# The end of attention: turns on VectorE and weighing on GpSimd in place of TensorE transposes, in a four-layer transformer kernel

## The chip, the cores and the metric

The kernel runs on one core of one Trainium2 chip (trn2). The metric is device time in microseconds of one launch. A core has TensorE (PE in the profile; its weight loads are PEld), VectorE (DVE), ScalarE (ACT), GpSimd (POOL) and SyncE (SP, which here only issues DMAs). They run side by side, each works through its own list of instructions in order, and they meet at semaphores.

## The reference, cut to what matters

Sixteen sequences of 256 tokens with 256 features pass four decoder layers; all four also look at a context of 77 rows per sequence. There are seven attentions, numbered 0 to 6 in the kernel: 0, 2 and 4 are self attention (0 and 2 causal, 4 with a mask that is handed in), 1, 3, 5 and 6 look at the context. Each has 16 heads of 16 features:

```python
q = x @ wq + bq;  k = ctx @ wk + bk;  v = ctx @ wv + bv      # ctx = x in self attention
scores = einsum('bhqd,bhkd->bhqk', q, k) / sqrt(16)
a = softmax(scores, axis=-1)
o = einsum('bhqk,bhkd->bqhd', a, v).reshape(B, N, 256)
x = x + o @ wo + bo                                          # with layer norms before or after
```

Since the rows of the softmax sum to one, the bias `bv` comes out as `o + bv`, and `(o + bv) @ wo + bo` is `o @ wo + (bv @ wo + bo)`. The layers also hold a feed-forward of 1024 features (two of them) and, in the second, a mixture of 8 experts of which 2 are chosen for each token. All matrices are float32; the scores are made with bfloat16 pieces (three to a number), so that they are as exact as float32 needs.

## The kernel before, in words

The program has three phases, one after the other, each a block with its own buffers. Phase a runs attentions 0 to 3 and the router for all 16 sequences, phase b the experts (39 groups of 256 rows), phase c attentions 4 to 6 and what follows. Within a and c up to seven sequences are under way at once.

The order on each engine is fixed before the program is built. `Plan.step` lists every step with the engine, a cost in microseconds, what it comes after (`after`), and which buffers it takes and gives back. `Plan.run` then plays them through: of all open steps it takes the one that can start first by its own costs, and of equals the more urgent one. The urgency is the length of the way to the end, a bonus for earlier sequences, and a number by stage from the table `AHEAD`, whose stages are named in `STAGES`. The costs, the takes and the table thus set the order; on the chip, each engine works it off and waits where something is late.

The end of one attention, before, in steps (lines of the kernel before):

- `pv` (L744): TensorE multiplies the exponentials with the values, each head's 16 values and a column of ones, so that the sum of the exponentials comes with it. Two steps for an attention, 8 heads each. Four heads stand side by side in the array (32 columns each); the outcome in PSUM has features on the partitions (32 for a head) and tokens along the free side.
- `raw` (L949): ScalarE copies each of the two banks to SBUF, 128x512.
- `turn_raw` (L754): TensorE transposes them, 4 blocks of 128x128 in each of two steps, so that tokens lie on the partitions.
- `recip`, `weigh` (L1112, L1118): VectorE takes the reciprocal of the sums and multiplies, for each half of the tokens.
- `turn_normed` (L763): TensorE transposes the outcome back, 4 blocks.
- `heads` (L955): ScalarE copies to SBUF and adds the value bias, two instructions.
- `out` (L780): TensorE multiplies with `wo`; `add` (L1124): VectorE adds the residual, to which GpSimd has added `bo` (`bias`, L1300) or which carries it in the shift of its layer norm (`shift`, L1290).

Other steps that the text speaks of: `qm` (L708, masks by L841 and L845) makes the scores for their maxima, `max` (L1087) takes these on VectorE, L1093 to L1106 split them in three bfloat16 pieces, `turn_shift` (L716) turns them, `turned_shift` (L931) copies, `shift_in` (L1352) is a DMA into the stack `qs`, and `km` (L728) makes the scores less the maxima; `exp` (L938) follows on ScalarE. `proj` is L686, `value_proj` L695, the feed-forward L796 and L780, the transposing of tokens L677 with the copy L911, and a norm's last step L1069.

## Time and profile before

| what | us |
|---|---|
| runs of the kernel before | 3228.45, 3234.26, 3242.9 (median 3234.26) |
| span of the profiled execution | 3229.7 |
| TensorE busy | 3020.0 (94%) |
| VectorE busy | 1570.3 (49%) |
| ScalarE busy | 1544.5 (48%) |
| GpSimd busy | 872.7 (27%) |
| mean granted clock of TensorE, share of full speed | 0.964 |

The profiled execution has no time of its own beside its span: 3229.7 us from the first to the last instruction, which is 4.6 us under the median of the runs. Phase a fills the span from 0 to about 1490 us, phase b to about 2070, phase c the rest.

A line of the profile names the line of the kernel, the engine, the operation and the tiles (out<-in). A float32 matmul shows as two instructions, so that four of them are an "x8"; a transpose shows as one. The duration of a matmul holds its way through the array and overlaps with the next; what a group of matmuls costs is told by the distance from its start to the start of the next, which is what the chain of waits gives.

### The profile page before, as it was taken

The page shows a single profiled execution, that of the slowest core. Times are in us where ns is not written, and L with a number is a line of the kernel's source. Part 1 is how long each engine was busy: PE and PEld are TensorE (multiplying, and loading weights), DVE is VectorE, ACT ScalarE, POOL GpSimd, SP SyncE. Part 2 cuts the span into 40 slices and gives each one's busy share as a digit, 9 for nine tenths or more (in the row PEclk, how much of TensorE's full clock was granted, in tenths as well). Part 3 has the DMA queues.
Part 4 walks back from the last instruction along what each step waited for, and adds up shares of the span by engine and source line. Part 5 has one row for each costly group of instructions (what it writes and reads, how often), then busy time and mean ns, then how long its engine had stood idle before and what let it go on. Part 6 is the DMA issues. An engine that isn't in the chain of part 4 may idle for free. (4 is left out here: it accounts for less than half of the span.)

```text
span 3229.7 us, 61791 instructions
## 1 busy us (share of the span) xinstructions
PE 3020.0 (94%) x23913; PEld 2459.4 (76%) x24016; DVE 1570.3 (49%) x4057; ACT 1544.5 (48%) x3403; POOL 872.7 (27%) x991
## 2 busy tenths in 40 slices
PE   7899999999999999876999999889999999999996
PEld 5788877788888777764888888656777777777774
DVE  4644454775556655452101011266566666666542
ACT  4555455565555566342222222145556555655552
POOL 2221213333223324222000000242234434433231
PEclk8999999999999999986999999899999999999997
DMA  9743536555645663724676665474435554656241
GB/s 165 110 64 45 62 50 84 96 79 76 79 63 76 81 84 67 193 44 159 209 230 210 199 205 192 98 111 65 51 60 73 77 77 63 82 75 79 40 56 25
DMA packets 394607, 319.34 MB, mean 99 GB/s; under 512 B 151711, under 2 KB 378271, under 8 KB 394303
## 3 DMA queue, kind: packets, MB, share of 16 engines
q1 hardware_dynamic: 371062, 276.77, 48.0%
q0 software_dynamic: 8272, 23.73, 3.0%
q10 hardware_dynamic: 14981, 14.89, 1.6%
q8 instruction: 190, 3.11, 0.5%
q14 instruction: 102, 0.84, 0.1%
HBM read 134.33 MB, written 37.22 MB: 53 GB/s over the span
## 5 line engine op out<-in xcount | busy, mean ns | idle before, releaser
L938 ACT ACTIVATE a_prob<-a_bank 128x512 f32<-128x512 f32 (+1 forms) x640 | 339.0, 599 | 108.7 <-PE a_bank L728 105.2
L1087 DVE TENSOR_REDUCE a_maxima<-a_bank 128x2 f32<-128x512 f32 (+3 forms) x576 | 338.2, 645 | 102.9 <-PE a_bank L708 102.6
L974 ACT ACTIVATE b_group_hidden<-b_bank,b_b 128x256 f32<-128x256 f32 x312 | 131.0, 471 | 421.6 <-PE b_bank L796 421.6
L938 ACT ACTIVATE c_prob<-c_bank 128x512 f32<-128x512 f32 (+1 forms) x512 | 263.2, 599 | 142.2 <-PE c_bank L728 140.4
L1087 DVE TENSOR_REDUCE c_maxima<-c_bank 128x2 f32<-128x512 f32 (+2 forms) x448 | 266.5, 638 | 95.2 <-PE c_bank L708 93.8
L796 PE MATMUL b_bank<-b_group_xt,b_w 128*128 128x256 f32 x1248 | 284.3, 381 | 0.8 <-DVE b_group_xt L1128 0.8
L780 PE MATMUL b_bank<-b_w,b_group_hidden 128*128 128x256 f32 x1248 | 275.8, 379 | 0.9 <-ACT b_group_hidden L974 0.9
L841 PE MATMUL a_bank<-a_causal_b,keep_identb 128*128 128x256 bf16 (+1 forms) x768 | 244.3, 318 | 34.2 <-DMA a_qs<-a_shift 25.0
L780 PEld LDWEIGHTS b_bank<-b_w,b_group_hidden 128*128 128x128 f32 x1248 | 237.0, 190 | 33.5 <-ACT b_group_hidden L974 1.3
L796 PEld LDWEIGHTS b_bank<-b_group_xt,b_w 128*128 128x128 f32 x1248 | 235.6, 191 | 32.0 <-DVE b_group_xt L1128 1.2
L1133 DVE TENSOR_TENSOR b_group_y<-b_bank,b_b 128x512 f32<-128x512 f32 x39 | 27.0, 692 | 364.8 <-PE b_bank L780 364.8
L728 PE MATMUL a_bank<-a_qs,a_ks 99*128 99x128 bf16 x1536 | 148.2, 225 | 0.0
L728 PEld LDWEIGHTS a_bank<-a_qs,a_ks 99*128 99x128 bf16 x1536 | 124.2, 101 | 23.2 <-issue 1.8
L708 PE MATMUL a_bank<-a_ks,a_qs 96*128 96x128 bf16 x1536 | 140.7, 220 | 0.0
L1124 DVE TENSOR_TENSOR a_tok<-a_bank,a_tok 128x512 f32<-128x512 f32 x80 | 55.1, 689 | 170.0 <-PE a_bank L780 169.8
L708 PEld LDWEIGHTS a_bank<-a_ks,a_qs 96*128 96x128 bf16 x1536 | 120.0, 98 | 22.7 <-issue 1.4
L780 PE MATMUL a_bank<-a_at_o,a_heads 128*128 128x256 f32 x512 | 131.2, 401 | 4.3 <-ACT a_heads L955 4.3
L1294 POOL TENSOR_TENSOR a_parts_q<-a_rest,a_parts_q 128x512 bf16<-128x512 f32 x64 | 74.3, 1161 | 224.8 <-ACT a_parts_q L927 224.7
L1286 POOL TENSOR_TENSOR c_tok<-c_tok,weights_row_L_xattn_ln_g 128x512 f32<-128x512 f32 x64 | 81.5, 1274 | 185.1 <-PE c_bank L677 185.1
L949 ACT ACTIVATE a_raw<-a_bank 128x512 f32<-128x512 f32 x128 | 76.4, 597 | 115.1 <-PE a_bank L744 114.5
L686 PE MATMUL a_bank<-a_xt,a_at_q 128*128 128x256 f32 x512 | 126.7, 391 | 3.2 <-ACT a_xt L911 1.6
L796 PE MATMUL c_bank<-c_xt,c_weights_f 128*128 128x256 f32 x512 | 122.4, 383 | 0.8 <-ACT c_xt L911 0.7
(239 smaller groups left out, 6475.9 us busy)
## 6 DMA issues: line engine op xcount, KB each, us to landing
b_w<-in_L_xattn_e_w SPq DMA_DIRECT2D x78, 1024.0 KB, 7.2
a_qs<-a_parts_q SPq DMA_DIRECT2D x384, 128.0 KB, 4.5
c_qs<-c_parts_q SPq DMA_DIRECT2D x288, 128.0 KB, 4.4
a_ks<-a_parts_k SPq DMA_DIRECT2D x192, 128.0 KB, 5.5
c_ks<-c_parts_k SPq DMA_DIRECT2D x96, 128.0 KB, 6.0
b_group_x<-sorted_in SPq DMA_DIRECT2D x39, 256.0 KB, 6.7
sorted_out<-b_group_y ACTq DMA_DIRECT2D x39, 256.0 KB, 5.1
sorted_in<-a_zeros SPq DMA_DIRECT2D x8, 1024.0 KB, 8.7
```

The source lines that it names most:

```text
L686: ins = pe.matmul(bank[:, 0, m * n:(m + 1) * n], weight[:, kt, m * P:(m + 1) * P], xt[:, kt, 0:n], start=(kt == 0), stop=(kt == KT - 1))
L708: ins = pe.matmul(bank[:, 0, to:to + m], qs[0:STACK, h, q * P:(q + 1) * P], ks[0:STACK, h, kt * P:kt * P + m], start=(at in CROSS), stop=( ...
L728: ins = pe.matmul(bank[0:kn, 0, to:to + m], ks[0:STACK + NPART, h, kt * P:kt * P + kn], qs[0:STACK + NPART, h, q0:q0 + m], start=(at in CR ...
L780: ins = pe.matmul(bank[:, 0, q * D:(q + 1) * D], heads[:, kt, q * P:(q + 1) * P], weight[:, kt, :], start=(kt == 0), stop=(kt == kts - 1))
L796: ins = pe.matmul(bank[:, 0, j * S:(j + 1) * S], weight[:, kt, f * P:(f + 1) * P], xt[:, kt, :], start=(kt == 0), stop=(kt == KT - 1))
L841: pe.matmul(blocks, k.identb, k.causal[:, keys_first, :].unsqueeze(1).broadcast_to([P, 4 // step, P]), start=True, stop=False)
L938: act.activation(prob[0:rows, first:first + cols], bank[0:rows, 0, 0:cols], ACT.Exp, scale=SCALE).then_inc(k.own(s), 1)
L949: act.activation(tile(s, "raw"), tile(s, "bank")[:, 0, :], ACT.Copy).then_inc(k.own(s), 1)
L974: ins = act.activation(hidden[:, f, :], bank[:, 0, j * S:(j + 1) * S], ACT.Gelu, bias=b1[:, f:f + 1])
L1087: v.tensor_reduce(maxima[:, q:q + qn, h:h + n].rearrange("p q h -> p h q"), bank[:, 0, 0:cols].rearrange("p (j q n) -> p j q n", j=n, q=qn ...
L1286: pool.tensor_tensor(x, x, over(k.gains[at][0]), ALU.mult).then_inc(k.own(s), 1)
L1294: pool.tensor_tensor(parts[:, 2, :, 0:n], rest[:, :, 0:n], parts[:, 1, :, 0:n], ALU.subtract).then_inc(k.own(s), 1)
```

## The change

The end of an attention now runs in five steps and without TensorE:

- `flip`: VectorE turns the 32x32 blocks of a `pv` bank (128x512) straight from PSUM into the buffer `flat`. As each head has 32 partitions, tokens then lie on partitions within a block. Two for an attention.
- `recip`: one reciprocal on VectorE for the whole attention.
- `weigh`: one multiplication on GpSimd, 128x512 in SBUF, into `normed`.
- `heads`: VectorE turns 32x32 blocks back, 128x512 from SBUF to SBUF. No bias is added.

Each block keeps its head's 16 features, so the order of features differs from before; the rows of `wo` and the value biases are laid out to fit (`paired`). The value bias is multiplied with `wo` once for each attention (`bias_out`, TensorE, two matmuls with the bias spread over the columns) and added to the row that holds `bo` or the norm's shift (`bias_fold`, VectorE). The buffers `raw` (four of 128x512) go, `flat` comes (two of 128x1024). The costs of `pv` in the plan rise, and all numbers of `AHEAD` are others.

```diff
-            plan.step("tensor", "pv", b, at, i, us=1.13 if at in CAUSAL else 1.35 if at in SELF else 0.5,
+            plan.step("tensor", "pv", b, at, i, us=1.3 if at in CAUSAL else 1.74 if at in SELF else 0.87,
...
-            plan.step("scalar", "raw", b, at, i, us=0.65, after=[("pv", b, at, i)], gives=["bank"], bank=pv, raw=raw)
...
-        plan.step("tensor", "turn_raw", b, at, q, us=0.44, after=[("raw", b, at, 0), ("raw", b, at, 1)]
...
-        plan.step("vector", "recip", b, at, q, us=0.28, after=[("turn_raw", b, at, q)], bank=bank, recip=recip)
-        plan.step("vector", "weigh", b, at, q, us=0.45, after=[("recip", b, at, q)] + ([("weigh", b, at, 0)] if q else []),
...
-    plan.step("tensor", "turn_normed", b, at, us=0.44, after=[("weigh", b, at, 0), ("weigh", b, at, 1)], takes=["bank", "heads"],
...
-    plan.step("scalar", "heads", b, at, us=0.87, after=[("turn_normed", b, at)], gives=["bank"],
...
+            plan.step("vector", "flip", b, at, i, us=0.69, after=[("pv", b, at, i)], gives=["bank"], bank=pv, flat=flat)
+    normed, heads, recip = ("normed", lab), ("heads", lab), ("recip", lab)
+    plan.step("vector", "recip", b, at, us=0.28, after=[("flip", b, at, 0), ("flip", b, at, 1)], takes=["recip"], flat=flat, recip=recip)
+    plan.step("gpsimd", "weigh", b, at, us=1.27, lag=0.1, after=[("recip", b, at)], takes=["normed"], gives=["flat", "recip"],
+              flat=flat, recip=recip, normed=normed)
+    plan.step("vector", "heads", b, at, us=0.69, after=[("weigh", b, at)], takes=["heads"], gives=["normed"],
+              normed=normed, heads=heads)
...
+SHIFT_AFTER = {"l1_1": 3, "l1_3": 4, "l2_1": 5, "l2_3": 6}
...
+def value_bias_steps(plan, at, ready, row_ready):
+    bank = ("bank", ("value_bias", at))
+    plan.step("tensor", "bias_out", -1, "bias", at, us=0.87, after=ready, takes=["bank"], bank=bank)
+    plan.step("vector", "bias_fold", -1, "bias", at, us=0.45, after=[("bias_out", -1, "bias", at)] + row_ready, gives=["bank"], bank=bank)
...
+    for at in (0, 1, 2, 3):
+        value_bias_steps(plan, at, [("load", -1, "a", at), ("load", -1, "a", "first")],
+                         [("fold", -1, "a")] if at == 3 else [bias_in(at)])
...
-AHEAD = {"a": {("shifts", 0): 0.1, ("shifts", 1): 2.4, ("shifts", 2): 0.3, ("shifts", 3): 0.8, ("shifts", "l0_ff"): -1.0,
+AHEAD = {"a": {("ends", 0): 0.6, ("ends", 1): 1.0, ("ends", 2): -0.2, ("ends", 3): -2.8, "ends": 0.4,
...
+        elif s.kind == "bias_out":
+            if phase == "a":
+                until.wait_ge(*done("load", -1, "a", s.part))
+                until.wait_ge(*done("load", -1, "a", "first"))
             until.wait_ge(*freed(s, "bank"))
+            bias, weight = k.biases[s.part][2], k.weights[s.part][3]
+            for kt in range(KT):
+                ins = pe.matmul(bank[:, 0, 0:D], bias[:, kt:kt + 1].broadcast_to([P, P]), weight[:, kt, :],
+                                start=(kt == 0), stop=(kt == KT - 1))
...
+        elif s.kind == "flip":
+            flat = tile(s, "flat")[:, s.part, :, :, :].rearrange("p b g c -> p g b c")
+            v.transpose(flat, tile(s, "bank")[:, 0, :].rearrange("p (g b c) -> p g b c", g=2, c=32)).then_inc(k.own(s), 1)
         elif s.kind == "recip":
+            v.reciprocal(tile(s, "recip"), tile(s, "flat").rearrange("p k b g c -> p (k b g) c")[:, :, HD]).then_inc(k.own(s), 1)
+        elif s.kind == "heads":
+            v.transpose(tile(s, "heads").rearrange("p k t -> p (k t)"),
+                        tile(s, "normed").rearrange("p n c -> p (n c)")).then_inc(k.own(s), 1)
...
+        elif s.kind == "weigh":
+            pool.tensor_tensor(tile(s, "normed"), flat[:, :, 0:HD],
+                               recip.unsqueeze(2).broadcast_to([P, recip.shape[1], HD]), ALU.mult).then_inc(k.own(s), 1)
```

First, TensorE at the very start of the program, before (L677 transposes the first tokens, L686 is their projection):

```order
L677 MATMUL a_bank<-keep_identity,a_tok 128x128 x4
L686 MATMUL a_bank<-a_xt,a_at_q 128x256 x4
L686 MATMUL a_bank<-a_xt,a_at_k 128x256 x4
L695 MATMUL a_bank<-a_at_v,a_xt 128x256 x4
L686 MATMUL a_bank<-a_ctx_t,a_at_k 128x77 x4
```

and after (L768 is `bias_out`, L689, L698 and L707 are the former L677, L686 and L695):

```order
L768 MATMUL a_bank<-a_at_o,keep_columns 128x256 x2
L689 MATMUL a_bank<-keep_identity,a_tok 128x128 x4
L698 MATMUL a_bank<-a_xt,a_at_q 128x256 x4
L698 MATMUL a_bank<-a_xt,a_at_k 128x256 x4
L707 MATMUL a_bank<-a_at_v,a_xt 128x256 x4
```

The folding of attention 0's bias, which needs the weights, stands ahead of the first transposing, which needs only tokens and the identity.

Second, the weights of attentions 2 and 3, which are loaded by ScalarE's DMA queue. TensorE after, where L740 and L756 are the former L728 and L744, L786 the former L780:

```order
L740 MATMUL a_bank<-a_qs,a_ctx_ks 77x256 x16
L698 MATMUL a_bank<-a_xt,a_at_q 128x256 x4
L728 MATMUL a_bank<-keep_identb,a_least_parts 96x128 x2
L786 MATMUL a_bank<-a_at_o,a_heads 128x256 x4
L756 MATMUL a_bank<-a_prob,a_ctx_values 32x256 x8
L768 MATMUL a_bank<-a_at_o,keep_columns 128x256 x2
L707 MATMUL a_bank<-a_at_v,a_xt 128x256 x4
L768 MATMUL a_bank<-a_at_o,keep_columns 128x256 x2
```

and ScalarE after, whose exponentials (L944) belong to the scores in the first row above:

```order
L944 ACTIVATE a_prob<-a_bank 77x512
L907 DMA a_at_q<-in_L_xattn_sa_wq 128x2x256
L907 DMA a_at_k<-in_L_xattn_sa_wk 128x2x256
L907 DMA a_at_v<-in_L_xattn_sa_wv 128x2x256
L907 DMA a_at_o<-in_L_xattn_sa_wo 128x2x256
L944 ACTIVATE a_prob<-a_bank 77x512
L907 DMA a_at_q<-in_L_xattn_ca_wq 128x2x256
L907 DMA a_at_k<-in_L_xattn_ca_wk 128x2x256
L907 DMA a_at_v<-in_L_xattn_ca_wv 128x2x256
L907 DMA a_at_o<-in_L_xattn_ca_wo 128x2x256
```

The loads stand between the same exponentials as before; new are the two L768 that stand few rows behind them on TensorE.

Third, TensorE in the even middle of phase c, from the turning of attention 6's maxima (L716) to its first scores (L728), before:

```order
L716 MATMUL c_bank<-keep_identb,c_least_parts 96x128 x2
L845 MATMUL c_bank<-c_weights_mask_q,keep_identb 128x512
L708 MATMUL c_bank<-c_ks,c_qs 128x256 x2
L796 MATMUL c_bank<-c_xt,c_weights_f 128x256 x4
L754 MATMUL c_bank<-keep_identity,c_raw 128x128 x4
L845 MATMUL c_bank<-c_weights_mask_q,keep_identb 128x512
L708 MATMUL c_bank<-c_ks,c_qs 128x256 x2
L754 MATMUL c_bank<-keep_identity,c_raw 128x128 x4
L780 MATMUL c_bank<-c_weights_f,c_qs 128x256 x16
L728 MATMUL c_bank<-c_qs,c_ctx_ks 77x256 x12
```

and after, with L728 and L740 in their places:

```order
L728 MATMUL c_bank<-keep_identb,c_least_parts 96x128 x2
L689 MATMUL c_bank<-keep_identity,c_tok 128x128 x4
L851 MATMUL c_bank<-c_weights_mask_q,keep_identb 128x512
L720 MATMUL c_bank<-c_ks,c_qs 128x256 x2
L851 MATMUL c_bank<-c_weights_mask_q,keep_identb 128x512
L720 MATMUL c_bank<-c_ks,c_qs 128x256 x2
L851 MATMUL c_bank<-c_weights_mask_q,keep_identb 128x512
L720 MATMUL c_bank<-c_ks,c_qs 128x256 x2
L698 MATMUL c_bank<-c_xt,c_weights_at_q 128x256 x4
L698 MATMUL c_bank<-c_xt,c_weights_at_k 128x256 x4
L740 MATMUL c_bank<-c_qs,c_ctx_ks 77x256 x12
```

The block of 16 feed-forward matmuls has moved out from between them, and the transposes L754 are gone.

## Rows read from the trace of the kernel before

**Rows 1.** The page, busy time of each engine over the span.

```profile
PE 3020.0 (94%) x23913; PEld 2459.4 (76%) x24016; DVE 1570.3 (49%) x4057; ACT 1544.5 (48%) x3403; POOL 872.7 (27%) x991
```

**Rows 2.** Stretches: from:to, length, busy time by engine, clock, DMA share, GB/s.

```profile
300.00:1400.00 1100.00, 1057.56 (x9917) 872.65 (x9916) 626.46 (x1757) 609.70 (x1342) 327.46 (x368) 0.98 0.54 81
2580.20:2646.80 66.60, 65.18 (x525) 51.48 (x532) 43.29 (x103) 38.08 (x84) 26.89 (x31) 1.00 0.55 75
```

**Rows 3.** Waits of TensorE: who, for whom, us in total, times, longest.

```profile
PE a_bank L841 <- DMA a_qs<-a_shift: 25.0, 10, 10.2
PE c_bank L728 <- DMA c_qs<-c_shift: 13.2, 3, 7.2
...
PE a_bank L763 <- DVE a_normed L1118: 4.3, 6, 1.1
```

**Rows 4.** Chain of waits in one period of phase c: start, us, what.

```profile
2589.82 0.22 PE c_bank L708 x2
...
2595.80 0.44 PE c_bank L754 x4
...
2604.95 0.40 PE c_bank L708 x2
...
2607.36 1.22 DVE c_least_parts L1106
```

**Rows 5.** Timeline of the start: start, us, engine, line, operation.

```profile
8.00 1.09 PE L677 MATMUL a_bank<-keep_identity,a_tok 128*128 128x128 f32 x4 [8.00 <-DVE a_tok L1069]
9.12 1.02 ACT L911 ACTIVATE a_xt<-a_bank,keep_columns 128x256 f32<-128x256 f32 x2 [1.33 <-PE a_bank L677]
10.50 3.78 PE L686 MATMUL a_bank<-a_xt,a_at_q 128*128 128x256 f32 x8 [1.41 <-DMA a_at_o<-in_L_xattn_m_proj_w]
```

**Rows 6.** Timeline of ScalarE's queue at the loads of attentions 2 and 3.

```profile
145.68 0.58 ACT L938 ACTIVATE a_prob<-a_bank 77x512 f32<-77x512 f32 x1
...
147.87 0.64 ACTq L901 DMA_DIRECT2D a_at_o<-in_L_xattn_sa_wo  x1
...
150.48 0.38 ACTq L901 DMA_DIRECT2D a_at_o<-in_L_xattn_ca_wo  x1
```

**Rows 7.** DMA issues: count, KB, us from issue to landing.

```profile
a_at_o<-in_L_xattn_sa_wo ACTq DMA_DIRECT2D x1, 256.0 KB, 10.1
...
a_at_o<-in_L_xattn_ca_wo ACTq DMA_DIRECT2D x1, 256.0 KB, 10.4
```

**Rows 8.** Groups of VectorE by shape: count, busy us, mean ns, idle before.

```profile
L1069 DVE TENSOR_SCALAR c_tok<-c_tok,c_moments,c_rstd 128x256 f32<-128x256 f32 x160 | 92.5, 619 | 33.6 <-POOL c_rstd L1279 33.4
...
L1069 DVE TENSOR_SCALAR a_tok<-a_tok,a_moments,a_rstd 128x256 f32<-128x256 f32 x128 | 54.7, 468 | 28.4 <-POOL a_rstd L1279 24.2 <-PE a_bank L677 3.6
...
L1118 DVE TENSOR_TENSOR c_normed<-c_bank,c_recip 128x256 f32<-128x256 f32 x96 | 40.7, 424 | 3.2
...
L1128 DVE COPY b_group_xt<-b_bank 128x512 f32<-128x512 f32 x39 | 27.0, 691 | 140.3 <-PE b_bank L677 140.3
...
L1112 DVE RECIPROCAL c_recip<-c_bank 128x16 f32<-128x16 f32 x96 | 24.1, 251 | 61.6 <-PE c_bank L754 61.1
```

**Rows 9.** Groups of GpSimd by shape, as rows 8.

```profile
L1300 POOL TENSOR_TENSOR a_tok<-a_tok,a_row_L_xattn_sa_bo 128x512 f32<-128x512 f32 x16 | 20.4, 1273 | 117.6 <-PE a_bank L677 117.6
```

**Rows 10.** Timeline of the last attention's end.

```profile
3206.59 1.93 PE L744 MATMUL c_bank<-c_prob,c_ctx_values 77*32 77x256 f32 x16 [0.74 <-ACT c_prob L938]
...
3214.06 3.78 PE L780 MATMUL c_bank<-c_weights_at_o,c_heads 128*128 128x256 f32 x8 [0.93 <-ACT c_heads L955]
```

**Rows 11.** Timeline of phase c: the maxima are turned and go to the stack.

```profile
2623.57 0.31 PE L716 MATMUL c_bank<-keep_identb,c_least_parts 128*96 128x128 bf16 x2
...
2624.59 0.75 SPq L1352 DMA_DIRECT2D c_qs<-c_shift  x1
```

**Rows 12.** Chain of waits, phase c: two such transfers, from issue to landing.

```profile
2326.95 8.01 DMA c_qs<-c_shift
...
3197.57 2.74 DMA c_qs<-c_shift
```

More of the change, by code:

```diff
@@ L263, in bias_step @@
 def bias_step(plan, b, at, x, out, source, after=(), takes=(), gives=()):
-    plan.step("gpsimd", "bias", b, at, us=1.27, lag=0.1, source=source, after=list(after) + [bias_in(at)], takes=takes, gives=gives,
+    plan.step("gpsimd", "bias", b, at, us=1.27, lag=0.1, source=source, after=list(after) + [bias_in(at) if at == "l0_ff" else ("bias_fold", -1, "bias", at)], takes=takes, gives=gives,
               x=x, out=out)
@@ L334, in attend_steps @@
               shift=shift, qs=qs)
+    flat = ("flat", lab)
     for g in range(H // 4):
```

123 lines of the change are left out of this document (55 added, 68 removed).

## The prediction

> **What bounds the kernel now.** I read the engines' busy time first: TensorE works 3020.0 of 3229.7 us, no other engine reaches half [rows 1]. A share over the span can hide stages, so the stretches come next. In the middle of phase a (300 to 1400 us) TensorE is busy 1057.56 of 1100 us. In the middle of phase c the kernel is periodic: 66.6 us for a sequence, of which TensorE works 65.18, VectorE 43.29, ScalarE 38.08 and GpSimd 26.89 [rows 2]. So there a microsecond taken from TensorE is a microsecond of the period, as long as nothing else comes late. The chain of waits says the same, as nearly all its pieces in a period are TensorE's; one is VectorE's, 1.22 us for an instruction on 32 columns [rows 4]. Last the waits: for the transfer that carries the maxima into the stack TensorE waits 25.0 us in phase a and 13.2 in c, one of them 10.2 us long; inside an attention's end the waits are short, the largest group 4.3 us in all [rows 3].
>
> **Part 1, the transposes go.** Four transposes of 128x128 hold the chain for 0.44 us [rows 4]. An attention has twelve, there are 7 x 16 = 112 attentions, so 336 x 0.44 = 147.8 us of TensorE go, 84.5 in phase a and 63.4 in phase c. Nothing lies beside them, so all of it counts: the period of phase c should fall from 66.6 by 3 x 1.32 = 4.0 to 62.6 us. Nothing is added to TensorE at an attention's end, the `pv` matmuls are the same.
>
> **Part 2, what it costs elsewhere.** No row shows the 32x32 turn. The nearest is VectorE's copy of a 128x512 bank, 691 ns [rows 8]; this I take, since the turn also reads and writes each element once. The lower end is the 424 ns of a 128x256 multiplication from PSUM (half the elements) [rows 8]; the upper, worked out from the copy, is four times 691, 2.8 us, if the turn read its blocks at a quarter of that rate. The Trainium skill ("Vector Engine (DVE) Microarchitecture Reference", section 3.8, the reshape front-end) says the 32x32 transpose sustains one element per cycle per lane; no row here shows it, and by it the price would be the copy's.
>
> VectorE loses 2 x (251 + 424) ns = 1.35 us an attention and gains two flips, a reciprocal and the turn back, 3 x 0.69 + 0.27 = 2.34 us [rows 8]. That is +1.0 us, so +3.0 in a period: 46.3 of 62.6 us, hidden behind TensorE. ScalarE loses two copies and two bias instructions. GpSimd gains one 128x512 operation, 1273 ns [rows 9], 142 us in all, and has 30.7 of 62.6 us in a period. All this is covered by TensorE's work while the order leaves it time. The way from the last `pv` to `out` becomes 0.69 + 0.27 + 1.27 + 0.69 = 2.9, with five handovers about 3.4 us. I counted TensorE's work between the two in the new order with the trace's own durations: in phase c the even part leaves 32, 21 and 7 us for attentions 4, 5 and 6; in phase a about 20 of 64 attentions have under 4.5 us, the least 2.3 but for the drain. They wait a few tenths each. TensorE's present waits inside the ends of attention, some 11 us (the largest group is the 4.3 of [rows 3]), go. I set the two against each other, at 0; the bounds are -11 and +20.
>
> **Part 3, the value bias.** Seven steps of two float32 matmuls. Three fall where TensorE is short: 3 x 0.87 = +2.6. The three of phase c stand ahead of everything at its start, where TensorE waits for other things: 0. The first stands ahead of the first transposing and waits for all four weights of attention 0. These landed at 10.50 us; the transposing ran at 8.00 [rows 5]. Now: weights 10.5, two matmuls at the start's slow clock 1.9 (half of the 3.78 of four), transposing 1.1, copy 1.0, so the projection starts at about 14.7 and not 10.5: +4. Waits of the first 75 us could take some of it back: 0 to 4.4.
>
> **Part 4, two loads that TensorE now waits for early.** The folding for attentions 2 and 3 stands on TensorE behind one projection, one `out` and one `pv` step from the scores whose first exponentials release the loads. Before, from the start of such an exponential (145.68) the last weights of attention 2 landed at 147.87 + 10.1 = 158.0, those of attention 3 at 150.48 + 10.4 = 160.9 [rows 6, 7]; that is 12.3 and 15.2 us later. TensorE's own work from there to the first folding is 1.75 + 1.73 + 0.11 + 1.73 + 1.0 = 6.3 us, less 0.5 for the start of the exponentials, so it stands for about 6.5 us; between the two foldings lie 2.7 us of work against 2.9 of landing. In the middle of phase a nothing gives that back: +7, bounds 0 (the loads find an idle queue) and 9.
>
> **Part 5, the order anew.** What can be counted: steps of transposes followed straight by bfloat16 matmuls fall from 210 to 85. After some of them the next pair takes 0.40 us and not 0.22 [rows 4], I take a third of 125 x 0.2 us: -8, bounds 0 and -25. The number of runs of `pv` steps stays (198 to 202). What I weigh against it is the room for the maxima's way, from L716 to the first scores of the same attention. From L716 to the DMA's issue it takes 1.0 us [rows 11], and the landing 2.74 us on an idle queue, up to 8.01 on a loaded one [rows 12], so 3.7 to 9. The order before left, in the even part of phase c, 7.1, 6.7 and 10.4 us for attentions 4, 5 and 6; the new one leaves 6.4, 5.8 and 5.2, since the feed-forward block has moved away. In phase a about 24 attentions have under 6 us, 17 before. There 17 such cases waited 25.0 us, 1.5 each [rows 3]; 7 more make 10, and I add 5 for phase c: +15, bounds -25 (the new order happens to meet no full queue) and +50.
>
> **Part 6, the drains.** Where one attention after the other ends the phase, latency counts. From the last `pv` (3206.59 + 1.93) to `out` (3214.06) it was 5.5 us [rows 10], now 3.4; 1.3 of the 2.1 are in part 1 already, the rest five times: -4.
>
> **The sum** is made in the span: 3229.7 - 147.8 + 2.6 + 4 + 7 - 8 + 15 - 4 = 3098.5. The median of the runs lies 4.6 above the span, so 3103 us, 4.1% less.
>
> **Rivals.**
> - *Waits eat the gain* (3150). The room of 5.2 to 5.8 us in phase c turns out short in each period, 1 us twice: 12 x 2 = 24 us more, and as much in phase a. For it: a wait of 10.2 us with a room once enough [rows 3]. Against it: rooms of 6.7 us met only one wait in the even part.
> - *GpSimd in VectorE's way* (3140). The same norm instruction takes 468 ns in phase a and 619 in c [rows 8], where GpSimd is busy 30% (327.46 of 1100) and 40% [rows 2], and the 1.22 us of L1106 [rows 4] fits an instruction held up. At 15 ns for each point and 9 points more, 160 instructions cost 22 us in c and some 15 in a, if none is hidden; most of VectorE's time is, so I give it little. The Trainium skill ("SBUF — State Buffer", section on who interferes with whom) has the rule: a VectorE instruction in a two-port mode, or one with two SBUF inputs, and a GpSimd instruction that reads SBUF shut each other out for a whole instruction; the two rows agree with it.
> - *The new order is better than its rooms* (3060). The waits for the maxima in phase a go (-25 in place of +15).
> - *The turn is slow, and VectorE becomes the bound* (about 3290). The period's VectorE work is 43.3 - 4.05 + 0.8 + 9X, with X the time of a turn. It passes the old 66.6 us at X = 2.95; at 3.3 us phase c loses 16 x 3 = 48 us against before, and phase a, whose 46 of 81 us a sequence grow by 12X - 4.3, just reaches its old length; with the drains 3290. It is slower from X = 3 on, just above my upper end of 2.8, at which it would come out level. Against it: reading and writing is all a turn does.
> - *Nothing comes of it* (3230): TensorE would have to wait 4 us more in each period, with 16 us of VectorE's time free. Only a chain of late flips that hold PSUM banks could do it.
>
> **Chances.** Forecast, 3070 to 3135: 0.62. Better order, 3030 to 3070: 0.13. Waits or GpSimd, 3135 to 3218: 0.18. Within half a per cent (16 us, about what a measurement tells from no change): 0.03. Slower: 0.04. So faster 0.93. The range of 8 in 10 is 3050 to 3175; it takes in part 5's -25 and +50 with the small terms' bounds, and most of both cases next to the forecast.
>
> **What would show it.** Right: no TensorE transposes but L689; TensorE busy less by some 150 us or more; the period in phase c near 62.6 with VectorE at 46; flips of 0.69 us; a wait of about 6 us before L768 near 150 us, and the first projection at 14 to 15 us. Wrong: flips over 1 us; TensorE waits for `heads` of over 20 us in all; waits for the maxima's transfer of over 80 us, against 38 before; a period of over 64 us.

## The result and the profile after

The changed kernel takes 3088.11 us (median of 4 runs, 3081.85 to 3092.99), the kernel before beside it 3232.86: a ratio of 0.955, 95% interval 0.9526 to 0.9574. The profiled run took 3081.85 us, the fastest of the four; its span is 3080.0. The forecast was 3103 us.

The page of the profile after, its line of busy times; it answers to [rows 1].

```profile
PE 2882.7 (94%) x22700; PEld 2320.2 (75%) x22700; DVE 1704.9 (55%) x4064; ACT 1335.1 (43%) x2955; POOL 985.5 (32%) x1103
```

TensorE has 1316 instructions fewer (by its weight loads, 24016 before) and 137.3 us less of busy time, and is still busy 94% of the span. The trace before lacks 103 matmul records; an estimate, at the mean of 3020.0 / 23913 = 0.13 us each, makes the true difference some 150 us. Then two stretches of the trace after, with the columns of [rows 2]: from:to, length, busy time of TensorE, its weight loads, VectorE, ScalarE, GpSimd, granted clock, DMA share, GB/s.

```profile
300.00:1400.00 1100.00, 1038.38 (x9771) 842.74 (x9768) 729.42 (x1848) 540.75 (x1197) 396.39 (x436) 0.96 0.54 84
...
2362.50:2425.00 62.50, 62.18 (x497) 47.58 (x497) 45.91 (x103) 32.73 (x72) 29.62 (x33) 1.00 0.49 80
```

Phase c repeats every 62.2 us, 66.5 before (from one transfer of maxima to the third after it). In a period TensorE waits 0.3 us. Phase a is less full: in its middle TensorE is idle for 61.6 of 1100 us, and its clock is 0.96, not 0.98. The first transposing of phase b shows how long phase a lasted: 1437.8 us, 1505.2 before. From the last one (1975.2, 2042.6 before) to the end are 1104.8 us, 1187.1 before. So phase a gave 67.4 us and phase c 82.3, and phase b nothing.

The waits of TensorE, the trace after; they answer to [rows 3]: who, for whom, us in total, times, longest.

```profile
PE a_bank L689 <- DVE a_tok L1064: 18.6, 15, 3.2
PE a_bank L728 <- DVE a_least_parts L1101: 14.3, 7, 4.7
PE a_bank L740 <- DMA a_qs<-a_shift: 12.8, 5, 3.7
...
PE c_bank L786 <- DVE c_heads L1116: 10.4, 7, 3.2
PE a_bank L847 <- DMA a_qs<-a_shift: 9.3, 6, 4.4
...
PE a_bank L786 <- DVE a_heads L1116: 6.6, 9, 2.1
```

The waits for the maxima's transfer are 22.8 us with the 0.7 of phase c, against some 40 before; those for the new end (`heads`) are 17.0.

The prices, in groups by shape: count, busy us, mean ns, idle before; they answer to [rows 8] and [rows 9].

```profile
L1108 DVE STREAM_TRANSPOSE a_flat<-a_bank 128x512 f32<-128x512 f32 x128 | 89.8, 706 | 61.1 <-PE a_bank L756 60.4
...
L1064 DVE TENSOR_SCALAR c_tok<-c_tok,c_moments,c_rstd 128x256 f32<-128x256 f32 x160 | 87.8, 590 | 18.0 <-POOL c_rstd L1283 17.9
...
L1305 POOL TENSOR_TENSOR a_normed<-a_flat,a_recip 128x512 f32<-128x512 f32 x64 | 67.9, 1061 | 124.6 <-DVE a_recip L1112 115.6 <-DVE a_heads L1116 9.0
...
L1116 DVE STREAM_TRANSPOSE a_heads<-a_normed 128x512 f32<-128x512 f32 x64 | 44.9, 701 | 31.5 <-POOL a_normed L1305 20.2 <-PE a_bank L786 11.2
...
L1112 DVE RECIPROCAL a_recip<-a_flat 128x32 f32<-128x32 f32 x64 | 22.5, 352 | 1.9
```

The turn takes 706 ns (0.69 us was taken), the weighing 1061 (1273), the reciprocal 352 (270).

### The profile page after: what moved, and what is told of

Read it like the earlier page. It is cut to its first block and busy times, and to the rows that moved or that the text cites. A ratio compares the mean times of both kernels' runs of the same rounds, so it can differ in the third digit from the quotient of the medians.

```text
span 3080.0 us, 58767 instructions
## 1 busy us (share of the span) xinstructions
PE 2882.7 (94%) x22700; PEld 2320.2 (75%) x22700; DVE 1704.9 (55%) x4064; ACT 1335.1 (43%) x2955; POOL 985.5 (32%) x1103
## 3 DMA queue, kind: packets, MB, share of 16 engines
q8 instruction: 180, 2.95, 0.5%
## 5 line engine op out<-in xcount | busy, mean ns | idle before, releaser
L944 ACT ACTIVATE a_prob<-a_bank 128x512 f32<-128x512 f32 (+1 forms) x640 | 332.9, 601 | 138.2 <-PE a_bank L740 133.9
L944 ACT ACTIVATE c_prob<-c_bank 128x512 f32<-128x512 f32 (+1 forms) x512 | 262.9, 600 | 126.6 <-PE c_bank L740 125.9
L1082 DVE TENSOR_REDUCE c_maxima<-c_bank 128x6 f32<-128x462 f32 (+2 forms) x448 | 263.2, 632 | 42.4 <-PE c_bank L720 42.0
L786 PE MATMUL b_bank<-b_w,b_group_hidden 128*128 128x256 f32 x1248 | 275.8, 379 | 0.9 <-ACT b_group_hidden L969 0.9
L786 PEld LDWEIGHTS b_bank<-b_w,b_group_hidden 128*128 128x128 f32 x1248 | 237.0, 190 | 33.5 <-ACT b_group_hidden L969 1.3
L786 PE MATMUL a_bank<-a_at_o,a_heads 128*128 128x256 f32 x512 | 133.8, 408 | 10.2 <-DVE a_heads L1116 6.6
L740 PE MATMUL a_bank<-a_qs,a_ks 99*128 99x128 bf16 x1536 | 142.6, 220 | 0.0
L698 PE MATMUL a_bank<-a_xt,a_at_q 128*128 128x256 f32 x512 | 134.6, 409 | 5.3 <-ACT a_xt L917 4.4
L740 PEld LDWEIGHTS a_bank<-a_qs,a_ks 99*128 99x128 bf16 x1536 | 120.5, 98 | 22.2 <-issue 0.8
L1317 POOL DMA_INDIRECT c_pair_y<-sorted_out,keep_rows x64 | 64.1, 1002 | 224.0 <-issue 208.5
L1290 POOL TENSOR_TENSOR c_tok<-c_tok,weights_row_L_xattn_ln_g 128x512 f32<-128x512 f32 x64 | 80.8, 1270 | 163.7 <-PE c_bank L689 163.6
L1108 DVE STREAM_TRANSPOSE a_flat<-a_bank 128x512 f32<-128x512 f32 x128 | 89.8, 706 | 61.1 <-PE a_bank L756 60.4
```

The source lines that it names most:

```text
L698: ins = pe.matmul(bank[:, 0, m * n:(m + 1) * n], weight[:, kt, m * P:(m + 1) * P], xt[:, kt, 0:n], start=(kt == 0), stop=(kt == KT - 1))
L740: ins = pe.matmul(bank[0:kn, 0, to:to + m], ks[0:STACK + NPART, h, kt * P:kt * P + kn], qs[0:STACK + NPART, h, q0:q0 + m], start=(at in CR ...
L786: ins = pe.matmul(bank[:, 0, q * D:(q + 1) * D], heads[:, kt, q * P:(q + 1) * P], weight[:, kt, :], start=(kt == 0), stop=(kt == kts - 1))
L944: act.activation(prob[0:rows, first:first + cols], bank[0:rows, 0, 0:cols], ACT.Exp, scale=SCALE).then_inc(k.own(s), 1)
L1082: v.tensor_reduce(maxima[:, q:q + qn, h:h + n].rearrange("p q h -> p h q"), bank[:, 0, 0:cols].rearrange("p (j q n) -> p j q n", j=n, q=qn ...
L1108: v.transpose(flat, tile(s, "bank")[:, 0, :].rearrange("p (g b c) -> p g b c", g=2, c=32)).then_inc(k.own(s), 1)
```

## Experiments

Beside each run stands its ratio to the kernel before, taken on the same chip, which is what is compared. The three that stand ahead of the last in the table ran on a chip where the kernel before took 3251 us, against 3232 to 3234 on the others. The last three columns are each from one profiled run and are not scaled by chip.

| kernel | median us | ratio, 95% interval | phase a | phase c | period of c |
|---|---|---|---|---|---|
| before | 3232.86 | 1 | 1505.2 | 1187.1 | 66.5 |
| after | 3088.11 | 0.955, 0.9526 to 0.9574 | 1437.8 | 1104.8 | 62.2 |
| new ends, old numbers | 3288.29 | 1.0176, 1.0161 to 1.0192 | 1507.9 | 1231.8 | 71.8 |
| old ends, new numbers | 3386.34 | 1.0462, 1.0433 to 1.049 | 1565.0 | 1280.8 | none |
| transposes put back | 3193.81 | 0.9876, 0.9859 to 0.9893 | 1496.4 | 1164.2 | 66.1 |
| value bias later | 3083.72 | 0.9537, 0.9521 to 0.9553 | 1438.2 | 1100.8 | |
| old numbers, maxima on ScalarE's queue | 3254.08 | 1.0066, 1.0043 to 1.0089 | 1502.8 | 1211.7 | |
| maxima on ScalarE's queue | 3092.72 | 0.9563, 0.9539 to 0.9588 | 1429.9 | 1124.1 | 63.3 |
| turns twice | 3178.81 | 0.9834, 0.9806 to 0.9863 | 1494.8 | 1142.7 | 64.7 |
| weighing on VectorE, order made anew | 3223.77 | 0.9979, 0.9961 to 0.9996 | 1506.8 | 1169.0 | |
| weighing on VectorE, same order | 3120.13 | 0.9603, 0.9585 to 0.9621 | 1454.9 | 1127.2 | 64.4 |
| weighing twice | 3125.90 | 0.9626, 0.9604 to 0.9648 | 1473.7 | 1112.7 | 62.3 |
| old pv costs in the planner | 3255.85 | 1.0018, 1.0004 to 1.0033 | 1504.2 | 1214.2 | |
| maxima on ScalarE's queue, phase a alone | 3073.97 | 0.9507, 0.949 to 0.9525 | 1430.6 | 1104.4 | 62.2 |

Phase a is the time to the first transposing of phase b, phase c that from the last one to the end, both from the trace. "Numbers" are the table AHEAD and the planned costs of the `pv` steps.

**One half of the change alone: the ends.**

```diff
 # the changed kernel, with these of the kernel before
-us=1.3 if at in CAUSAL else 1.74 if at in SELF else 0.87
+us=1.13 if at in CAUSAL else 1.35 if at in SELF else 0.5
-AHEAD = {"a": {("ends", 0): 0.6, ("ends", 1): 1.0, ...
+AHEAD = {"a": {("shifts", 0): 0.1, ("shifts", 1): 2.4, ...
```

> The changed kernel with the table AHEAD and the planned costs of the pv steps of the kernel before. So the ends of attention and the value bias are as after the change, and only the numbers that set the order are the old ones. Theory (the gain is the transposes that left TensorE, and the new order brings only the shorter waits for the maxima's transfer, 22.8 us after against about 40 before): 3088 + 17 = 3105 us, period of phase c within 0.5 us of 62.2, TensorE's waits for a_shift and c_shift together near 40. Rival A (the new numbers bring a large part): 3140 us or more, period over 63.5. Rival B (they bring nothing): 3085 to 3092.

All three missed: 1.8% slower than before, with 336 groups of transposes fewer. The waits of this kernel:

```profile
PE c_bank L844 <- DMA c_qs<-c_shift: 42.3, 10, 6.2
PE a_bank L840 <- DMA a_qs<-a_shift: 31.0, 7, 18.2
...
PE c_bank L733 <- DMA c_qs<-c_shift: 10.0, 4, 5.5
...
PE a_bank L733 <- DMA a_qs<-a_shift: 6.7, 4, 3.7
```

90 us of waits for the maxima against 22.8. One of them, in the chain of waits of the same kernel (start, us, what):

```profile
2551.22 0.60 SPq L1354
2551.86 0.61 SPq L1354
2552.52 8.83 DMA c_qs<-c_shift
2561.39 0.61 PE c_bank L844
2562.00 0.43 PE c_bank L733 x2
2562.43 0.43 PE c_bank L844
...
2564.89 0.22 PE c_bank L844
```

ScalarE had the turned maxima ready at 2550.48, SyncE issued three copies of parts first, and the transfer then took 8.83 us where [rows 12] had 8.01 and 2.74. Behind the wait each of these entries (one matmul of L844, or two of L733) takes 0.43 us, and 0.22 some 3 us later. The stretches around it, and ahead of them the flight of another transfer of the same period, columns as above:

```profile
2500.10:2506.10 6.00, 6.00 (x67) 3.78 (x66) 5.50 (x13) 1.58 (x3) 3.47 (x4) 1.00 0.06 9
...
2541.84:2552.52 10.68, 10.33 (x106) 7.58 (x105) 10.14 (x22) 6.53 (x15) 7.31 (x6) 1.00 0.97 118
2552.52:2561.35 8.83, 3.10 (x26) 2.31 (x22) 5.94 (x11) 2.62 (x6) 5.10 (x5) 0.80 1.22 111
...
2561.30:2564.60 3.30, 3.21 (x12) 1.68 (x13) 0.00 (x0) 1.62 (x3) 0.00 (x0) 0.50 1.30 107
```

The DMA share, last but one in a row, is 1.22 while the transfer is under way: the DMA engines are full. The granted clock, ahead of it, is 0.50 for 3.3 us after the wait of some 6 us: TensorE runs at the lower of its levels, 1.2 GHz. In the changed kernel the three transfers of a period are issued at the starts of these stretches:

```profile
2512.87:2518.87 6.00, 6.00 (x58) 4.24 (x50) 5.53 (x13) 1.87 (x4) 0.93 (x2) 1.00 0.96 104
2533.59:2539.59 6.00, 6.00 (x61) 4.16 (x59) 4.07 (x8) 3.64 (x9) 2.85 (x3) 1.00 0.35 98
2561.80:2567.80 6.00, 6.00 (x39) 5.07 (x37) 5.66 (x13) 2.98 (x7) 3.39 (x4) 1.00 0.10 28
```

0.96, 0.35 and 0.10 of the DMA engines, and TensorE waits for none. The room (TensorE's work between the turning of the maxima and the first scores that need them), which I had counted in the order, was almost the same: 5.5, 5.4 and 6.9 us in the slow order, 6.4, 5.8 and 5.2 in the good one. Within the slow period, too, the transfer of 2500.10 met a share of 0.06 and was not waited for, and the one of 2552.52, with about the same room, met 1.22 and was waited for 5.8 us. So in these periods the room does not tell the two orders apart, and what is on the DMA engines during the flight does. Part of the 5.8 us is also the issue, 2.0 us behind the turned maxima.

**The other half alone: the order.** The same two edits the other way round, on the kernel before.

> The kernel before with the new table AHEAD and the new planned costs of the pv steps, and nothing else. Counted in the order, phase c does not come to a fixed period under these numbers. Theory (the numbers fit the new ends and bring nothing by themselves): 3233 to 3265 us, TensorE busy within 10 us of 3020, since the 336 transposes per output half are all still there. Rival A (the order is worth some 17 us in any kernel, by shorter waits for the maxima): 3216. Rival B (the order carries a third or more of the gain): 3185 or less.

The theory's sign was right and its size was not: 4.6% slower. The waits for the maxima are 73.6 us (four groups, 23.3, 23.0, 14.3 and 13.0). TensorE's busy time is 3089.4 us, 69 more than before, at a mean clock of 0.947, for the same instructions (103 of them have no record in the trace before, which makes some 13 of the 69, an estimate from 0.13 us each). Rival A, an order that is good by itself, is out: the numbers fit one set of steps and costs.

**The transposes put back, in the changed kernel's own order.**

```diff
+            if s.kind == "out" and at in k.weights:
+                for i in range(12):
+                    pe.transpose(bank[:, 0, (i % 4) * P:(i % 4 + 1) * P], k.identf, k.identf)
             for q in range(QT):
```

> The changed kernel in its own order, with twelve 128x128 float32 transposes of the identity put back on TensorE in every attention's output step, behind its waits and ahead of its matmuls, into the same PSUM bank that the matmuls then overwrite. No wait is added. Theory (TensorE bounds the kernel nearly everywhere, so its time on the transposes counts in full): 1344 transposes at 0.11 us, +147.8: 3236 us, the time of the kernel before; period of phase c 62.2 + 3.96 = 66.2. Rival A (some of it lies beside waits for other engines): +110 to +130, 3198 to 3218. Rival B (the gain came from elsewhere): under +80, below 3170.

Rival A comes nearest. The ratio rises by 0.0326, which is 105 us of 3232.9, and not 148. (The phases below add up to 118 us: the profiled run was the slowest of this kernel's four, and that of the changed kernel the fastest of its four.) In phase c the price is nearly full: the period goes from 62.2 to 66.1, +3.9 where 3.96 was expected. In phase a the profile shows +58.6 where 84.5 was. Its middle stretch says why:

```profile
300.00:1400.00 1100.00, 1064.69 (x10099) 882.68 (x10097) 706.78 (x1771) 525.42 (x1166) 380.36 (x419) 0.98 0.53 82
```

The idle time falls from 61.6 to 35.3 us and the clock rises from 0.96 to 0.98: part of the transposes lay in waits for others, and with fewer waits the rest ran faster. And the kernel with all the transposes is still 1.2% faster than before. Between the two kernels, with nearly the same work on TensorE, lie 40 us. No run divides them: they hold the order, but also the shorter way through an end and the copies that ScalarE no longer makes (1544.5 us of busy time before, 1334.5 here). The period of phase c is only 0.4 us shorter than before, 6 us in 16 sequences, while phase c as a whole is 22.9 us shorter and phase a 8.8, so most of it lies elsewhere.

**The early steps of the value bias moved.**

```diff
+BEHIND = {0: ("proj", 0, 0, "k"), 1: ("value_proj", 0, 1, 0), 2: ("turn", 0, "l0_3", 0), 3: ("turn", 0, "l1_0", 0)}
-              takes=["bank"], bank=bank)
+              takes=["bank"], bank=bank, behind=[BEHIND[at]] if at in BEHIND else [])
```

> The changed kernel, in which the four value-bias steps of phase a stand later in TensorE's order: the first behind the first key projection, the third and fourth behind the first transposings of the feed-forward norm and of the second layer, when their loads have long landed. The rest of the order of phase a keeps 96% of its sequence, phase c all of it. Theory (the early steps made TensorE wait 5.2 us at the start and 3.2 + 0.4 us for the loads, with nothing that gives it back): the first projection at 10.5 us again, no wait of over 1 us before the value-bias matmuls, 3088 - 9 = 3079 us. Rival (the waits were covered and come back one step later, for the maxima or for ScalarE): within 3 us of 3088.

The intervals overlap. The waits in question are gone, but phase a is no shorter (1438.2 against 1437.8). They came back as others, in this kernel's waits (4.6 us and none in the changed kernel):

```profile
PE a_bank L702 <- DMA a_ctx_t<-in_ctx_t: 14.2, 4, 9.9
...
PE a_bank L702 <- DMA a_at_v<-in_L_xattn_cv_w: 13.0, 1, 13.0
```

By these waits the start is bound by its loads, wherever TensorE stands while they come. The 4 us are in phase c, whose order was not touched, and so are no effect that this edit explains.

**The maxima's transfer on ScalarE's queue**, under the old numbers and then in the changed kernel.

```diff
 # scalar_program, behind the copy of the turned maxima; SyncE issues it no more
+            until.wait_ge(*done("turned_shift", b, at))
+            into = k.plan.steps["shift_in", b, at, 0]
+            act.dma_start(tile(into, "qs")[STACK:STACK + NPART, :, :], tile(s, "shift")).then_inc(k.own(into), 16)
```

> The kernel with the new ends under the old numbers (measured 3288 us), in which the transfer of the maxima into the stack is issued by ScalarE, right behind its own copy of the turned maxima, and not by SyncE behind the copies of the parts. The order of every other instruction is the same. Theory (with the old numbers the maxima's transfer stands on SyncE's queue right behind three or four copies of 128 KB; its landings of 6.5 and 8.8 us and the slow matmuls behind such a wait are what the order costs): the landings fall toward 3 us, the waits for c_shift and a_shift from 90 to under 30 us, the granted clock from 0.944 to over 0.955: 3180 to 3210 us. Rival A (the 16 DMA engines are shared, so the bytes ahead delay it on any queue): landings of 5 us or more, 3260 to 3290. Rival B (the waits for the maxima are not what makes this kernel slow, it is the short room at the ends): waits for the maxima gone, and waits for heads up by as much, within 20 us of 3288.

By the ratios 36 us come back, of 202; the time lies above the theory's range and just below rival A's. Here are the four longest of its transfers between 2500 and 2800 us, from the chain of waits:

```profile
2545.72 8.75 DMA c_qs<-c_shift
...
2615.77 8.20 DMA c_qs<-c_shift
...
2683.78 8.62 DMA c_qs<-c_shift
...
2752.67 8.81 DMA c_qs<-c_shift
```

On SyncE's queue, under the same numbers, they took 8.12 to 9.29 us. So rival A holds for the landing, and what was won is the issue, which no longer stands behind the copies. The Trainium skill says that each DMA engine takes turns between the queues that have work, a packet at a time ("DMA: Bandwidth & Descriptors", section "Queues, rings and completion order"); from that I had expected a small transfer to land early from a queue of its own. In this case's trace it did not. The waits for the maxima's transfer fell from 90 to 43 us. But 127 us of idle time and 70 of busy time divide the slow order (on SyncE's queue) from the good one, and of the 127 only 67 are waits for that transfer. Of the other 60, 28 are longer waits for VectorE's taking of the maxima (33.3 us against 5.1), 16 for its norms (42.3 against 26.1) and 7 for `heads` (24.0 against 17.0). No run tests what each of them is worth.

> The same edit in the changed kernel: ScalarE issues the maxima's transfer. Theory (TensorE waits for it only 22 us in all here, since the new order leaves the queue free when it comes): 10 to 20 us less, 3070 to 3078. Rival A (the issue holds ScalarE 0.8 to 1.2 us, 112 times, and the exponentials behind it come later): 3090 to 3110. Rival B (the queue was never its delay): within 3 us of 3088.

Level with the changed kernel, and at 3092.72 us inside rival A's range; but its phases are not level: phase a is 7.9 us shorter, phase c 19.3 longer, where nothing was to be won and the period grew from 62.2 to 63.3 us. TensorE now waits six times in 400 us for ScalarE's copy of a transposed norm, 0.5 us each.

**The turns twice.** Each 32x32 turn is issued twice in a row into the same tile.

```diff
 # flip, and the turn back (heads) likewise; again() waits for the first before the second
-            v.transpose(flat, ...).then_inc(k.own(s), 1)
+            for i in range(2):
+                ins = v.transpose(flat, ...)
+                if i < 1:
+                    again(k, v, ins)
+            ins.then_inc(k.own(s), 1)
```

> The changed kernel in its own order, with each 32x32 turn on VectorE done twice in a row into the same tile: two flips and the turn back, 3 x 0.71 = 2.1 us more in an attention, 6.3 us in a period of phase c (45.8 to 52.2 of 62.2 us). The way from the last pv step to the output matmuls grows from about 3.9 to 6.0 us. Theory (VectorE is hidden in the period, the ends are not everywhere: by TensorE's work between the two in the order, the rooms fall short by 51 us more, 40 in phase a, 11 in c): 3088 + 51 = 3139, range 3115 to 3165, period of phase c still 62.2 to 63. Rival A (all is hidden): under 3100. Rival B (VectorE's lateness passes on to the maxima and to the norms, since one more microsecond of VectorE in ten makes each of its answers late): 3190 or more, period over 65.

+91 us, between theory and rival B. A period of phase c, and TensorE's waits in six of them:

```profile
2500.00:2564.70 64.70, 62.40 (x496) 47.35 (x495) 52.59 (x112) 32.93 (x72) 29.67 (x33) 1.00 0.50 77
```

```profile
PE c_bank L689 <- DVE c_tok L1070: 11.3, 7, 1.6
PE c_bank L728 <- DVE c_least_parts L1107: 4.5, 13, 0.4
```

VectorE has 12 us free in a period, and yet 6.3 us more of it cost 2.5. In this even part the waits are not for the ends but for the norm and for the maxima. Outside these periods TensorE does wait for the ends, over the whole run 52.2 us against 17.0:

```profile
PE a_bank L786 <- DVE a_heads L1127: 29.8, 24, 3.4
PE c_bank L786 <- DVE c_heads L1127: 22.4, 11, 5.4
```

The profiled run is 94 us longer than that of the changed kernel. TensorE's idle time is 71 us of it: 35 for `heads`, 20 for the norms, 7 for a bank that a flip holds, the rest in small pieces; its busy time is the other 23. The chain of waits of the changed kernel shows that the maxima were at their limit already:

```profile
2507.06 1.79 DVE c_maxima L1082 x3
...
2508.87 1.29 DVE c_maxima L1082 x2
...
2510.18 0.33 DVE c_least_parts L1088
...
2510.54 1.10 DVE c_least_rest L1092
```

From 2507.04 to 2512.12 the chain runs over VectorE, five microseconds of the period, though TensorE waits only 0.3.

**The weighing twice on GpSimd**, in the same manner.

```diff
-            pool.tensor_tensor(tile(s, "normed"), flat[:, :, 0:HD], ..., ALU.mult).then_inc(k.own(s), 1)
+            for i in range(2):
+                ins = pool.tensor_tensor(tile(s, "normed"), flat[:, :, 0:HD], ..., ALU.mult)
+                if i < 1:
+                    again(k, pool, ins)
+            ins.then_inc(k.own(s), 1)
```

> The changed kernel in its own order, with the weighing on GpSimd done twice in a row into the same tile: 1.06 us more of GpSimd in an attention, 3.2 us in a period of phase c (29.6 to 32.8), and as much more on the way through the end. Theory (only the longer way costs, where TensorE's work in the order does not cover it: 18 us more of shortfall in phase a, 4 in c): 3110, range 3098 to 3120. Rival A (a busier GpSimd also holds VectorE up): 3125 or more, VectorE's operations on 32 columns and its norm instruction longer by 10% or more. Rival B (all hidden): under 3095.

The ratio is 0.0076 over that of the changed kernel: +25 us, 3112 us on the chip of the changed kernel, as the theory had it. The profiled phases are 35.9 us longer in a and 7.9 in c; both hold what the slower chip adds (18 us for the kernel before), so phase a had most of the cost, but how much is not shown. The period is 62.3:

```profile
2500.00:2562.30 62.30, 61.25 (x488) 47.15 (x492) 46.44 (x102) 32.22 (x72) 32.86 (x36) 1.00 0.51 80
```

3.2 us more of GpSimd made VectorE's time 0.9 us longer (45.57 in a period of the changed kernel). The four instructions on 32 columns take 1.41 us in the mean of phase c, where they took 1.25 (13% more, part of rival A's sign); the norm's there stayed at 0.59 us. VectorE is held up, but in phase c that stays hidden. The Trainium skill ("SBUF — State Buffer", section on who interferes with whom) says that a VectorE instruction with two SBUF inputs and a GpSimd instruction that reads SBUF shut each other out for a whole instruction. The rows agree with it, and as a price it is small here.

**The weighing on VectorE**, first with the order made anew by the same numbers, then in the very order of the changed kernel.

```diff
 # first: the planner sees one step on VectorE (heads, 1.3 us), which weighs and turns back
-    plan.step("gpsimd", "weigh", b, at, us=1.27, ...
-    plan.step("vector", "heads", b, at, us=0.69, ...
+    plan.step("vector", "heads", b, at, us=1.3, after=[("recip", b, at)], ...
 # then: the planner sees the steps of the changed kernel, and only the emitted order differs
-            order[s.engine].append(s)
+            order[s.engine if s.kind != "weigh" else "vector"].append(s)
```

> The changed kernel with the weighing done by VectorE ahead of the turn back, and not by GpSimd; the order is made anew by the same numbers and keeps 65 to 74% of its sequence. An estimate of the weighing on VectorE is 0.69 us, by its other instructions on 128x512 elements, so VectorE has 47.9 of 62.2 us in a period and GpSimd 26.4 instead of 29.6. Theory (both engines are hidden, and only the order decides): 3080 to 3130, whichever way the order falls; period near 62.2. Rival A (GpSimd's instructions hold up VectorE's, so taking 112 of them away brings time): 3070 or less, L1092's successor near 200 ns instead of 469 in phase c. Rival B (any order that is not searched for loses as the old numbers did): 3150 or more.

> The changed kernel with the weighing on VectorE, as in the run before, but in the very order of the changed kernel: TensorE, ScalarE and SyncE issue what they did, and the weighing stands in VectorE's order where it stood in the common order of all engines. Theory (what made the run before 136 us slower is the new order that the planner laid, not the engine of the weighing): 3070 to 3105, with 3085 taken: the way through the end of attention is shorter by some 0.4 us (-8), VectorE has 77 us more work (+13, at the 0.17 us per us that doubling the turns leaves beside the ways), GpSimd's 119 us no longer hold VectorE up (-8). Rival A (the weighing belongs on GpSimd, since VectorE's time is short): 3120 or more. Rival B (GpSimd's hold of VectorE is a large cost): below 3065.

Ratios 0.9979 and 0.9603: the first meets rival B, the second is 3104.5 us on the chip of the changed kernel and inside the theory's range. The engine costs 0.0053, 17 us; the order that the planner made of it costs 0.0376, 122 us. In the same order L1092 takes 421 ns in the mean of phase c, 469 in the changed kernel, so GpSimd's hold on it eased little. The period is 64.4 us, 2.2 longer. VectorE works 46.5 of it, 0.9 more than in the changed kernel; TensorE works 61.9, as there, and waits 2.5 where it waited 0.3. The largest piece is a wait of 1.4 us for a bank that a flip holds, five times in 400 us:

```profile
PE c_bank L707 <- DVE c_flat L1108: 7.0, 5, 1.4
```

The changed kernel has no such wait in the same 400 us. The weighing now stands in the flip's way on VectorE; that this causes the wait is argued and not tested.

**The old costs of the `pv` steps with the new table.**

```diff
-us=1.3 if at in CAUSAL else 1.74 if at in SELF else 0.87
+us=1.13 if at in CAUSAL else 1.35 if at in SELF else 0.5
```

> The changed kernel with its own table AHEAD, but with the planned costs of the pv steps of the kernel before (1.13, 1.35 and 0.5 us in place of 1.3, 1.74 and 0.87). Nothing else changes; the planner lays another order from it, which in phase c does not come to a fixed period. Theory (the gain of the order lies in this one order and not in what the numbers stand for, so one that was not searched for loses some 100 us or more): 3190, range 3150 to 3260, waits for a_shift and c_shift over 60 us. Rival (the table carries the gain, and costs of a few tenths do no harm): within 25 us of 3088.

The theory held in its size, at 4.9% over the changed kernel and level with the kernel before (by the ratio 3239 us on the chip of the changed kernel). The waits for the maxima are 40.3 us in all, not over 60, so there too they are a part only.

**The version that beats both**: the transfer on ScalarE's queue in phase a alone.

```diff
 # scalar_program, behind the copy of the turned maxima
+            if phase == "c":
+                continue
+            until.wait_ge(*done("turned_shift", b, at))
...
 # sync_program
-        elif s.kind == "shift_in":
+        elif s.kind == "shift_in" and phase == "c":
```

> The changed kernel, in which ScalarE issues the maxima's transfer in phase a alone; in phase c SyncE does, as before. With both phases so, the run was within half a per cent of the changed kernel, but its trace has phase a 7.9 us shorter (1429.9 against 1437.8) and phase c 19.3 longer (1124.1 against 1104.8, from the last transposing of phase b to the end). Theory (the two parts are real and independent: in phase a the transfer lands earlier, in phase c, with no wait to win, the issue holds ScalarE up each time): 3080 us, phase a near 1430, phase c near 1105, ratio to the kernel before 0.953. Rival (such differences of a few us are only the chance fall of the waits): within 3 us of 3088, ratio 0.955.

3073.97 us, ratio 0.9507 (0.949 to 0.9525), 0.4% under the changed kernel, with intervals that all but touch. Phase a is 1430.6 and phase c 1104.4 us, each where the theory put it. The waits for maxima in phase a fell from 22.1 to 12.2 us.

## Why the prediction was right, and where it was not

The time, the sign and the period of phase c (62.6 forecast, 62.2 measured, VectorE 45.6 for 46.3, GpSimd 29.6 for 30.7) came out. That the time came out within 15 us is in part luck, since two errors nearly cancel. The transposes were worth 105 us and not 148, 43 less. The other terms of the sum were to add 17 us; the measured gain of 145 us, without these 105, leaves them taking 40 away, 57 the other way.

- **Part 1, the transposes.** The mechanism is right and in phase c the size too (3.9 of 3.96 us a period). "Nothing lies beside them, so all of it counts" fails in phase a, where TensorE is idle 4 to 6% of the time: 58.6 of 84.5 us there. In place of -148 the sum needed about -105. The step was carried from a periodic stretch with no waits to one with many.
- **Part 2, the prices.** Turn and reciprocal were close, the weighing 0.2 us too dear. Waits at the ends: 17 us for `heads`, against 11 that went; the forecast of 0 holds within its bounds. "Hidden behind TensorE" is true of GpSimd in the even part of phase c and was wrong of VectorE. VectorE was 73% busy, and 230 us more of it cost 91. An estimate from the weighing twice (25 us for 1.06 us on the way) gives the longer way 50 of them and the engine's own lateness 40; the waits of the doubled turns have 35 for `heads`, so the division is not shown. On the same scale the rival of the slow turn was too kind: I put its break-even at X = 2.95 us, and an estimate from the doubled turns, 0.71 us more for 91 of the 145, gives 1.8. The rival of GpSimd in VectorE's way took 15 ns on the norm for each point of GpSimd's share. In phase c the share rose from 40 to 48% and the norm fell from 619 to 590 ns; in phase a, from 30 to 36%, it rose from 468 to 509. The scale does not hold in phase c.
- **Part 3 and part 4, start and loads.** The projection stood at 15.67 us, 5.2 later than before where 4 was forecast, and outside "14 to 15": the first L768 waited for the row of output biases, which landed at 11.63, and not for the weights of 10.50 that I had read. The waits before the two later L768 were 3.2 and 0.4 us instead of 6 (my rows give 6.0 in all; the 7 in the sum has no row behind it), and the first of them stood near 169 us and not near 150. But +4 and +7 were to be 0: with both taken away phase a stayed as it was. The rows, answering to [rows 5] and to the wait of part 4:

```profile
11.63 2.08 PE L768 MATMUL a_bank<-a_at_o,keep_columns 128*128 128x256 f32 x4 [11.63 <-DMA a_row_L_xattn_m_proj_b<-in_rows]
13.50 1.06 PE L689 MATMUL a_bank<-keep_identity,a_tok 128*128 128x128 f32 x4
15.67 3.78 PE L698 MATMUL a_bank<-a_xt,a_at_q 128*128 128x256 f32 x8 [1.11 <-ACT a_xt L917]
...
168.69 2.07 PE L768 MATMUL a_bank<-a_at_o,keep_columns 128*128 128x256 f32 x4 [3.22 <-DMA a_at_o<-in_L_xattn_sa_wo]
```

- **Part 5, the order.** This step failed. I gave it -8 and +15, worked out from the room ahead of the first scores; the waits for the maxima went from 40 to 22.8 us, down where +15 had them go up. The kernel with the transposes back in is 40 us faster than before, though how much of that is the order is not shown. The range of -25 to +50 held this, not what the order decides at large: with the same ends, an order by the old numbers is 6.6% slower, one by the old `pv` costs 4.9%. Rival "nothing comes of it" had a chance of 3% for a chain of late flips; with the old `pv` costs in the planner the kernel came out level with the one before, so what could have made it true is an order that was not fitted. I read the new order's rooms, but not what each of its transfers meets.
- **Part 6, the drains.** From the last `pv` to `out` it is 3.11 us (3.4 forecast), from 3060.21 + 1.07 to 3064.39.

## What to carry to other kernels

Where one engine is busy all of a periodic stretch, work taken from it is worth its full time (3.9 of 3.96 us here); where it idles 5%, count on less (58.6 of 84.5), and the trace of each stretch tells which. An order made by a planner belongs to the exact steps and costs that it was fitted to: an edit and its order are one change, and to judge the edit alone, keep the order of all other instructions, as in the last forms of the weighing and of the turns. For a small transfer on which the next stage waits, look at what the DMA engines carry while it flies, and not only at the room that it has.

## What the runs showed of the hardware

- A wait costs twice. After 6 us of idle time TensorE ran for 3.3 us at 0.50 of its clock. Over the whole kernel the same 22700 matmuls are busy 2882.7 us in the good order and 2952.8 in the slow one (mean clock 0.965 and 0.944): 70 us that no list of waits shows.
- A transfer of 24 KB that TensorE waited for took 8.1 to 9.3 us from SyncE's queue and 8.2 to 8.8 from ScalarE's, with the DMA share at 1.17 to 1.22 during the flight, and 2.74 us with it at 0.03 [rows 12].
- A turn of 32x32 blocks of a 128x512 float32 bank is as fast out of PSUM (706 ns) as between two tiles in SBUF (701), and costs what the plain copy of the same size does, 691 ns [rows 8]. The Trainium skill ("Vector Engine (DVE) Microarchitecture Reference", section 3.8) gives the turn one element per cycle and lane; a turn at the price of a copy agrees with it.
- GpSimd's product of 128x512 elements with a factor broadcast over 16 takes 1061 ns. Its sum with a row of 256 numbers, read once for each half of the 512, takes 1273 [rows 9], and the product with such a row 1270 in the changed kernel.
